# Two conditioned attention layers: FiLM with tokens on partitions, its rows through DRAM, its result turned by DMA, and a new preparation

## The reference

```
xn = layernorm(x) * ln_w + ln_b
q, k, v = xn @ Wq + bq, xn @ Wk + bk (+ mask), (xn @ Wv + bv) * mask
layer 0 (8 heads of 32):   y = softmax_features(q) @ (softmax_tokens(k)^T v)      linear attention
layer 1 (16 heads of 16):  y = softmax(q k^T + mask) @ v                          full attention
scale, shift = split(silu(cond) @ W_emb + b_emb)                                  one row of 2 x 256 per sequence
h = (layernorm(y) * ln2_w + ln2_b) * (1 + scale) + shift                          FiLM
x = x + silu(h) @ W_out + b_out
```

## Time and profile before

| | us |
|---|---|
| median of three runs | 843.88 (841.26 to 845.1) |
| the profiled execution | 841.51 |
| its span | 839.7 |

### The profile page before, as it was taken

How to read it: one execution, slowest core, us unless ns; L and a number is a source line. 1 busy time by engine, 2 the same in 40 slices (tenths; PEclk the granted TensorE clock), 3 DMA queues, 4 the chain that set the end, 5 groups by cost and what they waited for, 6 DMA issues and landing times. The chain is left out here.

```text
span 839.7 us, 27295 instructions
## 1 busy us (share of the span) xinstructions
PE 808.4 (96%) x9421; PEld 572.3 (68%) x9421; DVE 730.7 (87%) x1482; ACT 725.4 (86%) x1666; POOL 691.9 (82%) x1020
## 2 busy tenths in 40 slices
PE   9998889999999999999999999999999999999995
PEld 3487666777776777777776777777777677665643
DVE  5879789999988889989999889899989898899962
ACT  5688668899898989889899889998989889999995
POOL 8658999999879999888899978998987987796523
PEclk9599999999999999999999999999999999999999
DMA  7311454544334443434354442444444332354301
GB/s 223 88 29 40 115 137 105 125 98 124 94 96 118 121 112 98 105 95 103 101 124 108 118 118 67 127 97 93 120 112 114 107 78 74 109 113 116 111 21 38
DMA packets 149316, 85.97 MB, mean 102 GB/s; under 512 B 87478, under 2 KB 141852, under 8 KB 149180
## 3 DMA queue, kind: packets, MB, share of 16 engines
q1 hardware_dynamic: 149180, 84.23, 39.8%
HBM read 39.52 MB, written 25.79 MB: 78 GB/s over the span
## 5 line engine op out<-in xcount | busy, mean ns | idle before, releaser
L1292 DVE TENSOR_REDUCE NM<-banks 128x4 f32<-128x1024 f32 x256 | 306.2, 1211 | 38.3 <-PE banks L823 36.8
L1781 ACT ACTIVATE wraw<-banks 128x1024 f32<-128x1024 f32 x154 | 157.0, 1037 | 13.9 <-PE banks L834 12.6
L2014 POOL TENSOR_TENSOR rs<-ve,nhalf 128x2 f32<-128x2 f32 x128 | 91.4, 716 | 33.1 <-ACT ve L1656 32.4
L1781 ACT ACTIVATE PX<-banks 128x1024 f32<-128x1024 f32 x102 | 104.3, 1039 | 10.2 <-PE banks L834 10.0
L698 PE MATMUL banks<-wo,SH 128*128 128x256 f16 x768 | 95.8, 275 | 5.4 <-POOL SH L2091 5.1
L2091 POOL TENSOR_TENSOR SH<-ST,SH 128x512 f16<-128x512 f32 x64 | 75.3, 1179 | 27.8 <-ACT SH L1745 27.6
L823 PE MATMUL banks<-SK,SQ 51*128 51x256 f16 x1024 | 92.8, 272 | 4.3 <-DMA SQ<-scr 2.6
L834 PE MATMUL banks<-SQ,SK 53*128 53x256 f16 x1024 | 92.8, 272 | 3.4 <-DVE Y L1311 0.9
L698 PE MATMUL banks<-wv,ZT 128*128 128x256 f16 x768 | 93.4, 273 | 0.1
L698 PEld LDWEIGHTS banks<-wo,SH 128*128 128x128 f16 x768 | 72.4, 98 | 22.3 <-POOL SH L2091 7.8
L847 PE MATMUL banks<-wraw,V 128*32 128x256 f32 x1232 | 87.1, 384 | 0.1
(11 more groups left out here) (187 smaller groups left out, 1907.8 us busy)
## 6 DMA issues: line engine op xcount, KB each, us to landing
scr<-AB SPq DMA_DIRECT2D x64, 256.0 KB, 2.3
X<-in_x_dram SPq DMA_DIRECT2D x32, 256.0 KB, 2.9
SK<-scr SPq DMA_DIRECT2D x64, 128.0 KB, 2.7
SQ<-scr SPq DMA_DIRECT2D x64, 128.0 KB, 2.5
out_dram<-wemb SPq DMA_DIRECT2D x32, 256.0 KB, 2.3
SK<-scr SPq DMA_DIRECT2D x64, 64.0 KB, 2.7
SQ<-scr SPq DMA_DIRECT2D x64, 64.0 KB, 2.6
wemb<-in_L_cond_W_emb_dram SPq DMA_DIRECT2D x1, 1024.0 KB, 6.3
```

The costliest lines, as they stand in the source:

```text
L1292: V.tensor_reduce(NMe[:, c, :, 2 * g:2 * g + 2], banks[:, n:n + 2, :].rearrange("p a (h m) -> p a h m", m=T), AX.X, ALU.max, negate=True). ...
L1781: A.activation(px(v % 5), banks[:, n:n + 2, :].rearrange("p a n -> p (a n)"), ACT.Exp, scale=r_uu).then_inc(S["exp"])
L2014: G.tensor_tensor(rs[:, b % 2, l, :], ve[:, b % 2, l, :], nhalf[:, :], ALU.pow).then_inc(S[f"r{l}"])
```

## The change

FiLM stays with tokens on partitions in both layers, and the preparation is redone.

- `yn0` and `yn1` move from GpSimd to VectorE and write HH (two instructions of 128x256 each). YN is gone.
- The scaled FiLM rows (512 values a batch) are written to DRAM once (`fw0`, `fw1`), and each batch's row is read into all 128 partitions (`fr0`, `fr1`, tile FR, one buffer a layer).
- GpSimd multiplies and adds them: `fa` and `fb`, HH = HH * row, HH = HH + row, one instruction of 128x512 each.
- `th` is one Tanh over 128x512 in SBUF, with its scale from a register. `st` is as before.
- `sh` writes the high part into SHL in the layout of the DMA transpose, `sl` the low part in two instructions; `sT0` and `sT1` (SyncE) turn SHL into SHT, and the output products read SHT. `y0T` and `y1T` are gone, and their two PSUM uses.
- `h0`, `h1` move from GpSimd to ScalarE (one instruction each), `c0` too (two instructions, with `m0` for its bias).
- Preparation: 30 warm-up matmuls, other load order, FiLM rows made on 32 partitions from PSUM (`film_token`), fills by broadcast DMA from a small constant, the bias row's three parts on VectorE at their place.
- All lists, BANK and FREED are written anew.

```diff
-HOT = 44
+HOT = 30
+            def load_g(l):
+                s = SRC[l]
+                for v, a, z in ((s[7], 0, 2 * D), (s[8], 2 * D, 3 * D), (s[9], 3 * D, 4 * D)):
+                    e.dma_start(film_src[l][:, a:z], v.unsqueeze(0).to_broadcast([NB, z - a])).then_inc(l_g[l], 16)
+            def film_out(l):
+                ready(e, f"film{l}")
+                e.dma_start(fmd[l], film_row[l]).then_inc(l_fm[l], 16)
+            def film_in(b, l, i):
+                e.wait_ge(S[f"fb{l}"], b)
+                if b == 0:
+                    e.wait_ge(l_fm[l], 16)
+                e.dma_start(FR[:, i].rearrange("p a n -> p (a n)"), fmd[l, b].unsqueeze(0).to_broadcast([P, 2 * D])).then_inc(d_fr[l][b % 2], 16)
+            def turn_out(b, l, i):
+                e.wait_ge(S[f"sl{l}"], b + 1)
+                e.wait_ge(S[f"o{l}"], b)
+                e.dma_start(SHT[:, i].rearrange("p j k (t n) -> p (j k t) n", t=2),
+                            SHL[:, i].rearrange("p j k t n -> p (j k t n)"), transpose=True).then_inc(d_s[l][b % 2], 16)
+            def fill_q():
+                e.wait_ge(l_fil, 16)
+                for h in range(2):
+                    e.dma_start(SQ[HALF * h + ROW1:HALF * h + ROWM, :, :, :].rearrange("p r h t -> p (r h t)"),
+                                fil.unsqueeze(0).to_broadcast([ROWM - ROW1, 3 * H1 // 2 * T])).then_inc(l_fq, 16)
...
-            def y0T(b):
-                e.wait_ge(S["yn0"], b + 1)
-                clear(e, "gy0T", b)
-                transposes(home("gy0T", b), YN[:, 0]).then_inc(S["y0T"])
             def o0(b):
-                e.wait_ge(S["sl0"], b + 1)
+                e.wait_ge(d_s[0][b % 2], 16 * (b // 2 + 1))
...
-                tok_major(bank(home("go0", b)), SH[:, 0], W["o", 0]).then_inc(S["o0"])
+                tok_major(bank(home("go0", b)), SHT[:, 0], W["o", 0]).then_inc(S["o0"])
...
+            def yn0(b):
+                e.wait_ge(S["r1"], b + 1)
+                e.wait_ge(S["st0"], b)
+                for t in range(2):
+                    i = V.tensor_scalar(HH[:, 0, t, :], Y[:, 0, t, :], nm[:, b % 2, 1, t:t + 1],
+                                        rs[:, b % 2, 1, t:t + 1], ALU.add, ALU.mult)
+                i.then_inc(S["yn0"])
...
             def th0(b):
-                th_of(b, 0)
+                e.wait_ge(S["fb0"], b + 1)
+                e.wait_ge(S["st0"], b)
+                A.activation(TH[:, 0], HH[:, 0], ACT.Tanh, scale=r_t[0]).then_inc(S["th0"])
             def sh0(b):
+                e.wait_ge(S["st0"], b + 1)
+                if b >= 1:
+                    e.wait_ge(d_s[0][(b - 1) % 2], 16 * ((b - 1) // 2 + 1))
+                A.activation(SHL[:, 0, 0].rearrange("p k t n -> p t k n"),
+                             ST[:, 0].rearrange("p t (k n) -> p t k n", k=2), ACT.Identity).then_inc(S["sh0"])
...
+            def m0(b):
+                for t in range(2):
+                    i = A.activation(nmr[:, b % 2, 0, t:t + 1], nm[:, b % 2, 0, t:t + 1], ACT.Copy,
+                                     scale=rs[:, b % 2, 0, t:t + 1])
+            def c0(b):
+                e.wait_ge(S["m0"], b + 1)
+                e.wait_ge(S["z0"], b)
+                for t in range(2):
+                    i = A.activation(Z[:, 0, t, :], X[:, b % 3][:, t, :], ACT.Identity, bias=nmr[:, b % 2, 0, t:t + 1],
+                                     scale=rs[:, b % 2, 0, t:t + 1])
...
+            def fa0(b):
+                e.wait_ge(S["yn0"], b + 1)
+                e.wait_ge(d_fr[0][b % 2], 16 * (b // 2 + 1))
+                G.tensor_tensor(HH[:, 0], HH[:, 0], both(FR[:, 0, 0, :]), ALU.mult).then_inc(S["fa0"])
+            def fb0(b):
+                e.wait_ge(S["fa0"], b + 1)
+                G.tensor_tensor(HH[:, 0], HH[:, 0], both(FR[:, 0, 1, :]), ALU.add).then_inc(S["fb0"])
             def sl0(b):
+                e.wait_ge(S["sh0"], b + 1)
+                for k in range(2):
+                    i = G.tensor_tensor(SHL[:, 0, 1, k], ST[:, 0].rearrange("p t (k n) -> p t k n", k=2)[:, :, k, :],
+                                        SHL[:, 0, 0, k], ALU.subtract)
```

More of the change, by code:

```diff
@@ new lines @@
+    "gt_w0": "1",
+    "gcnd": "0",
+    "gt_o0": "2",
+    "ga_w0": "1",
+    "gbb1": "0",
+    "gpm": "3",
+    "gfx0": "4",
+    "ga_o0": "2",
+    "grow3": "5",
+    "gv0": "32045514472300043634202031652337",
+    "gt_f0": "4",
+    "gbb0": "0",
+    "gq0": "53013106736116732623440464661361",
+    "ga_f0": "4",
+    "gk0": "01342325567234102112375723040110",
+    "gt_w1": "6",
+    "grw": "7",
+    "gkt": "67352122536204705013141645174400",
+    "ga_w1": "0",
+    "gqt": "27036557652176247324517740512761",
@@ L320, in bass_cond_seq @@
         d_out = [sem(f"d_out{i}") for i in range(2)]
+        d_fr = [[sem(f"d_fr{l}{i}") for i in range(2)] for l in range(2)]
+        d_s = [[sem(f"d_s{l}{i}") for i in range(2)] for l in range(2)]
+        l_g = [sem(f"l_g{l}") for l in range(2)]
+        l_fm = [sem(f"l_fm{l}") for l in range(2)]
+        l_rt = [sem(f"l_rt{l}") for l in range(2)]
         i_v, i_g = sem("i_v"), sem("i_g")
@@ L490, in bass_cond_seq @@
         at_col = lambda n: banks[:, home("gcol"), n:n + 1]
-        at_film = lambda l, m: banks[:, home(f"gfm{l}"), m * NB:(m + 1) * NB]
+        film_src = (low(SQ, 1), wemb[1][0:NB, 2:4, :].rearrange("p k n -> p (k n)"))
+        film_row = [wemb[l][0:NB, 0, :] for l in range(2)]
+        film_tmp = [wemb[l][0:NB, 1, :] for l in range(2)]
         ctx.enter_context(nc.allow_non_contiguous_dma(reason="vectors of 256 with features on partitions"))
@@ L989, in cond_rows @@
                     t = PE.matmul(at_conds(l), csT[:, k, :], wemb[l][:, k, :], start=(k == 0), stop=(k == 3))
-                t.then_inc(C["PE"])
-            def film(l):
-                ready(e, f"fy{l}", "cst")
-                clear(e, f"gfm{l}", 0)
-                for m in range(4):
-                    t = PE.transpose(at_film(l, m), wemb[l][0:NB, 0, m * P:(m + 1) * P], ident[0:NB, 0:NB])
                 t.then_inc(C["PE"])
@@ L1475, in mb0, with p3_ @@
                 V.tensor_copy(mb3[:, 2, :], mbf[:, 0, :]).then_inc(C["DVE"])
+            def p3_():
+                ready(e, "row3", "w0p", "pa", "cst")
+                follow(V.tensor_scalar(arow, at_row(3)[0:3, :], iu[0:3, 1:2], None, ALU.mult))
+                for i in range(2):
+                    follow(V.tensor_copy(augs[0:3, :], arow))
+                    follow(V.scalar_tensor_tensor(out=arow, in0=augs[0:3, :], scalar=asg[:, i:i + 1], in1=arow, op0=ALU.mult,
+                                                  op1=ALU.add))
+                V.tensor_copy(augs[0:3, :], arow).then_inc(C["DVE"])
             def csl_():
@@ L1648, in _ @@
             r_un, r_q, r_k, r_uu = (e.alloc_register(n) for n in ("r_un", "r_q", "r_k", "r_uu"))
+            r_t = [e.alloc_register(f"r_t{l}") for l in range(2)]
             def mean_of(b, l):
@@ L2100, in c1 @@
                 centred(b, 1, X1[:, b % 2])
-            def h1(b):
-                high(b, 1)
             def z1(b):
@@ L2137, in r3, with fa1, fb1 @@
                 norm(b, 3)
-            def yn1(b):
-                e.wait_ge(S["r3"], b + 1)
-                e.wait_ge(S["y1T"], b)
-                apply(b, 3, YN[:, 1], Y[:, 1], "yn1")
-            def sl1(b):
-                sl_of(b, 1)
+            def fa1(b):
+                e.wait_ge(S["yn1"], b + 1)
+                e.wait_ge(d_fr[1][b % 2], 16 * (b // 2 + 1))
+                G.tensor_tensor(HH[:, 1], HH[:, 1], both(FR[:, 1, 0, :]), ALU.mult).then_inc(S["fa1"])
+            def fb1(b):
+                e.wait_ge(S["fa1"], b + 1)
+                G.tensor_tensor(HH[:, 1], HH[:, 1], both(FR[:, 1, 1, :]), ALU.add).then_inc(S["fb1"])
+            def sl1(b):
+                e.wait_ge(S["sh1"], b + 1)
+                for k in range(2):
+                    i = G.tensor_tensor(SHL[:, 1, 1, k], ST[:, 1].rearrange("p t (k n) -> p t k n", k=2)[:, :, k, :],
+                                        SHL[:, 1, 0, k], ALU.subtract)
+                i.then_inc(S["sl1"])
             def cst():
```

1291 lines of the change are left out of this document (628 added, 663 removed), and 196 rows, old and new, of the table FREED.

## The result

The kernel after takes 865.9 us (862.8 to 867.8, 4 runs) against 843.9 (841.3 to 845.1, 4 runs): ratio 1.026, 95% interval [1.022, 1.030]. It is 22 us slower where 18 us faster was forecast, and outside the range. All times are medians of fast runs; one run of `fr_act`, 1.8% above the fastest of that kernel, is a slow one and is left out.

The account below looks back on a forecast made before the run. TensorE bounds the kernel before; VectorE would bound after. Steady part -13, start -8, end +3 sum to -18 us: 841.5 becomes 823.5, or 826 us for the median; own range 813 to 837, 8-in-10 range 808 to 847.

Parts of the forecast that it names:

- TensorE, 23.4 to 22.5 us a batch: Steady part: TensorE loses the eight transposes of normalised y per batch, falling from 23.4 to 22.5 us.
- VectorE, +1.5 to 23.0: Steady part: VectorE gains four `yn` instructions, 1.5 us a batch, rising from 21.5 to 23.0 (22.3 to 23.3).
- the 0.17 meant for contention: VectorE's `yn`: 0.17 us for sharing SBUF with GpSimd, added to 0.27 for the first of a pair.
- A batch is the fullest engine over 0.99: Steady part: VectorE at 99% makes a batch 23.2 us instead of 23.7, -13 us over 25.3 periods.
- GpSimd +0.3, "does not bound": Steady part: GpSimd's lost and gained work nets +0.3 us a batch, to 21.2, and does not bound.
- SyncE's queue at nothing: SyncE's transfers: four more issues a batch, about 3.3 us of issuing, costed at nothing in the main case.
- third rival: SyncE's queue: turns waiting for GpSimd block its head and delay loads, +34 us, 860 us (848 to 875); 12 in 100.
- The start, -8 us: Start: fewer warm-up matmuls, no film transposes, clock and fill gains sum to -8 us (0 to -16).
- The 4.0 us for 14 warm-up matmuls: Start: cutting the warm-up from 44 to 30 matmuls saves 4.0 us.
- its least case: Start: the bound of 0 gain, if weights land late and the clock drops in the gap.
- The end, +3 us: End: the chain from last Y to output product grows from 9.4 to 12.6 us, +3 us (0 to +7).
- The fourth rival: VectorE: each `yn` waits for GpSimd's running operation, +0.45 us; VectorE 24.4 us a batch, 862 us; 8 in 100.

Follow-up runs that it names:

- fr_act: Kernel after, with the FiLM row loads issued by ScalarE behind the tanh instead of by SyncE's list: 872.8 us, 1.036.
- no_yn: Kernel after, with the four TENSOR_SCALARs a batch that normalise y left out, GpSimd multiplying raw y: 849.1 us, 1.008.
- before_load: Kernel before, with four extra TENSOR_SCALARs of 128x256 a batch on VectorE, written to an unread scratch tile: 889.9 us, 1.056.
- before_stats: Kernel before, with six extra bn_stats a batch on VectorE, written to an unread scratch tile: 884.2 us, 1.050.
- no_fb: Kernel after, with GpSimd's FiLM addition of each layer left out: 845.7 us, 1.006.
- yn0_pool: Kernel after, with layer 0's normalisation of y put back on GpSimd ahead of the FiLM product: 873.1 us, 1.036.
- before_half_yn: Kernel before, with GpSimd normalising only the first half of y's tokens from batch 1 on: 841.5 us, 0.998.
- pow_fb: Kernel after, with GpSimd's FiLM addition of each layer replaced by two narrow GpSimd powers: 858.7 us, 1.021.
- hot44: Kernel after, with 44 instead of 30 warm-up matmuls on TensorE: 863.3 us, 1.024.
- before_hot30: Kernel before, with 30 instead of 44 warm-up matmuls on TensorE: 842.9 us, 1.000.

## Why the prediction was wrong

- **TensorE, 23.4 to 22.5 us a batch:** 22.8. Right in kind; it was no longer the bound.
- **VectorE, +1.5 to 23.0:** this step failed. It came to 23.7. The `yn` groups are busy for (17.9 + 17.4) us in 400, 2.15 us a batch; ST's mean went from 800 to 994 ns over the run (+0.4 a batch) and the second part of the row maxima from 393 to 560 (+0.2). These rows add up to 2.7; records of neighbours overlap more than before, and VectorE as a whole rose by 2.2. An undisturbed pair takes 0.74 us, two make the 1.5 forecast; but the single instruction is 0.41, not 0.27, so the 0.17 meant for contention was used up by its bare cost, and the right size of the pair was luck. The 0.7 us above it are waits behind GpSimd. I priced them by the contention that ST had and left out that ST and its neighbours would wait more. It is not `yn` that makes them wait: without it ST's mean is 1087 in the middle (`no_yn`), and with a like load in the kernel before it is 715. It is what GpSimd now does beside them, or the new order; no run takes those two apart.
- **A batch is the fullest engine over 0.99:** this failed as well. 23.7 / 0.97 = 24.4. The two together, 0.7 and 0.5 us, are the miss of 1.2 us a batch, some 30 us in 25 batches; the start (7) and the end (1) bring it near the 40 between 826 and 866. `before_load` and `before_stats` show that the fullest engine is no ceiling: with VectorE at 93% and TensorE at 94 to 96% an added us of VectorE cost 0.5 to 0.7 us of the batch (1.7 for 2.46 and 1.3 for 2.45 at the batch lengths; 0.6 and 0.5 over the whole run). In the kernel after, `no_yn` gave back 0.25 for each us; why there is a factor of two between them is open.
- **GpSimd +0.3, "does not bound":** 21.6 us, near the 21.2 forecast. But `no_fb` and `yn0_pool` show that its work has a price in the kernel after, which it had not before (`before_half_yn`). The forecast looked at the load, not at the place: `fa` and `fb` stand between `yn` and ST, and VectorE waits behind them. Which of these makes the price, `pow_fb` did not settle.
- **SyncE's queue at nothing:** this term was mis-sized too: 12 us for the transfers, 7 of them the rows' loads, 4 the end. The third rival's place (waits at the head of the queue) does not show: line 524, the turns, waits 20.3 us for GpSimd over the run, not 57, and line 519, the loads, 18.6. The scratch write's landing went from 2.3 to 3.6 us and is 2.6 without the loads; whether bytes or order made that, `fr_act` did not settle.
- **The start, -8 us:** this failed, -0.7 came of it. The 4.0 us for 14 warm-up matmuls were nothing (`hot44`, `before_hot30`): waits for loads, and in the kernel after the lower clock, took them back, which the forecast had only as its least case. The rest of the rebuilding brings the first product 10.4 us sooner, and 0.7 of it reaches the row maxima. From 60 to 150 us VectorE is busy 85.9 of 90 us (81.7 before), and the granted clock of TensorE is 0.92 (1.00 before); which of the two holds the filling up no run isolated.
- **The end, +3 us:** +4.2. The chain to the last product is 12.3 us against 12.6 forecast (9.4 before), right with its terms. Not forecast was that TensorE, idle for 6.70 us, would do the last product at the lower clock, +1.3 us.

The fourth rival, at 8 in 100, had the mechanism, the wait for the instruction that runs, and a time (862) near the measured one. I had set it low on ST's median, 57 ns above its least. That median was of one order of the lists: ST mostly fell beside nothing that it waits for. In the kernel after the same instruction's median is 269 ns above its least. That its time fits is luck: it had +0.45 us for each `yn`, where the mean, 565 ns, is 0.16 above the undisturbed one, and VectorE at 24.4 where it is 23.7; the lower fill (0.97 in place of 0.99), the transfers and the start make up for it. The Trainium skill's rule of the exclusive lock (SBUF — State Buffer, "Who interferes with whom") is borne out by the trace of after in the seven and seven cases under XB, and in the nine XB that started under an ST. The runs do not bear out that these waits are the whole price: they are VectorE's 0.7 us, and `before_stats`, whose added instructions never wait, is nearly as slow as `before_load`.
